# One-core decoder layer on Trainium2: where the gate products, the tile plan and the expert registers stand

## What is computed

```python
x = x + recurrence(layernorm(x))                     # stage A
x = x + cross_attention(layernorm(x), ctx)           # stage B: 16 heads, 77 keys
xf = layernorm(x)
gate_scores = xf @ gate_W + gate_b                   # [tokens, 4]
topk_scores, topk_idx = top_k(gate_scores, 2)
weights = softmax(topk_scores)
expert = LN(relu(LN(xf @ W1[e] + b1[e])) @ W2[e] + b2[e])    # stage C, for each e
x = x + sum_k weights[k] * expert[topk_idx[k]](xf) + xf
```

## Time and profile before

| what | value |
|---|---|
| median of 3 runs | 1238.64 us (1235.35 to 1240.6) |
| the profiled execution, its own time | 1244.41 us |
| its span, first to last instruction | 1242.6 us |
| PE busy | 1177.0 us, 95% of the span |
| DVE, ACT, POOL busy | 930.3, 731.6, 455.7 us |
| mean granted TensorE clock | 0.975 |

### The profile page before, as it was taken

The page is one execution under the profiler, slowest core; times in us unless marked ns, Lnnn a source line. Parts: engine busy times, 40 slices in busy tenths (PEclk is TensorE's granted clock), DMA queues, the critical chain, the costliest instruction groups (busy, mean ns, idle before and its releaser), DMA issues.

```text
span 1242.6 us, 24523 instructions
## 1 busy us (share of the span) xinstructions
PE 1177.0 (95%) x6041; PEld 991.0 (80%) x6042; DVE 930.3 (75%) x2196; ACT 731.6 (59%) x2114; POOL 455.7 (37%) x410
## 2 busy tenths in 40 slices
PE   6999999999879999999999989987999999999993
PEld 5878888888768888888888867866888888888882
DVE  6888888887745777877878676666777777777773
ACT  4323333233457758676676662655777777777773
POOL 4030000000033323545445254355655555555542
PEclk9999999999979999999999898899999999999997
DMA  8664544444620113041131325888555444444432
GB/s 273 209 161 144 194 160 152 169 152 165 200 69 1 44 60 103 11 136 67 35 103 42 129 40 127 299 225 226 86 86 82 83 84 84 81 80 84 84 65 38
DMA packets 76069, 143.90 MB, mean 116 GB/s; under 512 B 20460, under 2 KB 24752, under 8 KB 74117
## 3 DMA queue, kind: packets, MB, share of 16 engines
q1 hardware_dynamic: 56704, 101.60, 25.0%
q0 software_dynamic: 18464, 39.14, 17.3%
q10 hardware_dynamic: 837, 2.41, 0.6%
HBM read 78.83 MB, written 67.83 MB: 118 GB/s over the span
## 4 chain that ended last, share of the span: by engine, by line
PE 72%; DVE 9%; issue 8%; DMA 5%; ACT 2%; POOL 2%; DVEq 1%; another core or an unknown queue 0%; POOLq 0%; ACTq 0%; SPq 0%
PE banks L1049 26%; PE banks L670 13%; PE banks L735 6%; PE banks L875 6%; PE banks L865 5%; DMA out<-rows,scatter_rows 4%; PE banks L834 4%; PE banks L851 3%; PE banks L891 2%; PE banks L1077 2%; PE banks L1061 2%; DVE operands L1486 2%; DVE rows L1557 2%; PE banks L883 1%; DVE rows L1570 1%
## 5 line engine op out<-in xcount | busy, mean ns | idle before, releaser
L1049 PE MATMUL banks<-operands 128*128 x1608 | 392.3, 399 | 18.3 <-DVE operands L1486 11.7
L1049 PEld LDWEIGHTS banks<-operands 128*128 128x128 f32 x1608 | 299.9, 190 | 82.9 <-DVE operands L1486 14.4
L670 PE MATMUL banks<-operands 128*128 128x512 f32 (+2 forms) x1224 | 294.0, 397 | 3.6 <-DVE operands L1486 3.6
L670 PEld LDWEIGHTS banks<-operands 128*128 128x128 f32 (+1 forms) x1224 | 228.5, 194 | 49.4 <-DVE operands L1486 3.8
L1486 DVE TENSOR_TENSOR operands<-banks,operands 128x512 fp32r<-128x512 f32 (+3 forms) x328 | 218.6, 683 | 53.3 <-ACT operands L1141 48.7
L1141 ACT ACTIVATE operands<-banks 128x512 fp32r<-128x512 f32 (+3 forms) x328 | 192.1, 607 | 111.9 <-PE banks L865 45.2
L1262 ACT ACTIVATE rows<-banks,score_shift 128x77 f32<-128x77 f32 x512 | 162.3, 372 | 29.6 <-DVE score_shift L1708 28.9
L1141 ACT ACTIVATE operands<-rows 128x512 fp32r<-128x512 f32 (+3 forms) x79 | 55.2, 708 | 168.5 <-DVE rows L1557 135.4
L1411 ACT ACTIVATE banks<-banks,param_cols 128x128 f32<-128x128 f32 x268 | 99.0, 429 | 86.1 <-PE banks L1077 84.1
L2457 POOL DMA_INDIRECT out<-rows,scatter_rows x67 | 106.6, 1590 | 112.1 <-DVE rows L2196 68.8
L2381 POOL TENSOR_TENSOR rows<-rows,score_rec 128x1232 f32<-128x1232 f32 x32 | 72.0, 2252 | 157.9 <-DVE score_rec L1716 157.9
(11 more groups left out here) (178 smaller groups left out, 1718.2 us busy)
## 6 DMA issues: line engine op xcount, KB each, us to landing
expert_parts<-operands SPq DMA_DIRECT2D x32, 512.0 KB, 3.4
operands<-expert_parts SPq DMA_DIRECT2D x8, 2048.0 KB, 10.1
rows<-in_x SPq DMA_DIRECT2D x8, 1024.0 KB, 5.8
rows<-in_L_ffn_W SPq DMA_DIRECT2D x32, 256.0 KB, 3.8
x_rows<-rows SPq DMA_DIRECT2D x8, 1024.0 KB, 4.3
rows<-x_rows SPq DMA_DIRECT2D x8, 1024.0 KB, 6.0
xf_rows<-rows SPq DMA_DIRECT2D x32, 256.0 KB, 2.5
out<-rows SPq DMA_DIRECT2D x32, 256.0 KB
```

What stands on the lines that cost most here:

```text
L670: last = nc.tensor.matmul(dst, stationary(a, k), moving(b, k), start=(t == 0 and k == 0), stop=(t == len(terms) - 1 and k == n_k - 1))
L1049: last = nc.tensor.matmul(dst, stationary[:, a, k, :], weights[:, bass.ds(e, 1), w, a2, k, :].rearrange("p e f -> p (e f)"), start=False, ...
```

## The change

It has five parts.

1. In every turn from 1 to 6 the gate products of tiles 0 and 1 stand ahead of the queries of head group 3 instead of behind them, and those of tile 2 right behind these queries.
2. In the last turn the gate of chunk 6 was one block of 16 instructions at the end. Now tile 0 stands there, and tiles 1, 2 and 3 between halves of the first two projections of the tail. The group `g` moves from `MM_LAST` to `TAIL`, behind `o0`, so `o1` and the groups behind it change banks, and `prime(m1_bank[1])` waits for the read of `r` instead of `o3`. On DVE `gate_bias` and `choose` of that chunk move behind the first `x2_rows` of the tail.
3. In tile 0 of stage C the gate products of chunk 7 are two blocks of 8 instructions, the second within the first product of tile 2.
4. `plan_early(1)` moves on DVE from the start of the last turn to just before `plan_early(2)`.
5. The experts of tiles 0 to 2 are read into registers early: on PE in the last turn, on ACT ahead of its first fill. On DVE those reads move from tile 1 to tile 0.

```diff
-        MM_LAST = "o0 o1 r v0 o2 v1 o3 v2 v3 g".split()
+        MM_LAST = "o0 o1 r v0 o2 v1 o3 v2 v3".split()
...
-        TAIL = {id(T_ORDER): "xf0 xf1 xf2 xf3".split(), id(MM_ORDER): "o0 o1 o2 o3 r".split()}
+        TAIL = {id(T_ORDER): "xf0 xf1 xf2 xf3".split(), id(MM_ORDER): "o0 g o1 o2 o3 r".split()}
...
-        def tiles_of(engine, tile):
-
-
-            around = [None] * 2
+        def tiles_of(engine, tile, known=()):
+
+
+            around = [None] * 2 + list(known)
...
-            def project(c, at, j):
-
-                mm_free(at, f"o{j}")
-                for m in range(KC):
+            def project(c, at, j, parts=range(KC)):
+
+                if 0 in parts:
+                    mm_free(at, f"o{j}")
+                for m in parts:
...
-                last.then_inc(mm_done, 1)
+                if KC - 1 in parts:
+                    last.then_inc(mm_done, 1)
...
                 probs_to_keys(c, 3, (0, 1))
+                if back:
+                    gate_scores(c, (0, 1))
                 queries(c + 1, c, 3)
                 if back:
-                    gate_scores(c, (0, 1))
+                    gate_scores(c, (2,))
                 probs_to_keys(c, 3, (2,))
-                if back:
-                    gate_scores(c, (2,))
                 scores(c + 1, 1, (0, 1))
...
                 probs_to_keys(c, 3, (2,))
+                pe.wait_ge(plan_ready, 1)
+                first_experts.extend(expert_at(pe, i) for i in range(3))
                 xf_to_features(c - 1, c, 2)
...
-                gate_scores(c)
+                gate_scores(c + 1, (0,))
...
-            def first_product(i, u, e):
+            def first_product(i, u, e, between=None):
...
                 expert_product(m1_bank[u], e, 0, xT, (0, 1))
+                if between is not None:
+                    gate_products(tail_bank, tail, between).then_inc(tail_gate_done, 1)
                 pe.wait_ge(cx_lo, i + 1)
...
-                    gate_products(tail_bank, tail, range(TPC)).then_inc(tail_gate_done, 1)
+                    gate_products(tail_bank, tail, range(2))
...
             last_turn(last)
-            for j in range(TPC):
+            project(last, tail, 0, (0, 1))
+            gate_scores(tail, (1,))
+            project(last, tail, 0, (2, 3))
+            gate_scores(tail, (2,))
+            project(last, tail, 1, (0, 1))
+            gate_scores(tail, (3,))
+            project(last, tail, 1, (2, 3))
+            for j in range(2, TPC):
                 project(last, tail, j)
             positions(last - 1, tail, "r")
-            pe.wait_ge(plan_ready, 1)
-            first_product(0, 0, expert_at(pe, 0))
+            first_product(0, 0, first_experts[0])
...
-            pe.wait_ge(mm_read, mm_num(tail, "o3") + 1)
+            pe.wait_ge(mm_read, mm_num(tail, "r") + 1)
             prime(m1_bank[1])
-            first_product(1, 1, expert_at(pe, 1))
+            first_product(1, 1, first_experts[1])
...
             act.wait_ge(primed, 1)
-            fill_first(0, 0, expert_at(act, 0))
+            first_experts = [expert_at(act, i) for i in range(3)]
+            fill_first(0, 0, first_experts[0])
...
-                plan_early(1)
                 x2_rows(c - 1, c, 0)
...
                 read_positions(c)
+                plan_early(1)
                 plan_early(2)
...
                 slots(c - 2, c, aside=1)
-                gate_bias(c)
-                choose(c - 1, c)
...
                     count(NCH - 1)
+                    coming()
...
             x2_rows(last, tail, 0)
+            gate_bias(tail)
+            choose(last - 1, tail)
             count(last - 1)
```

More of the change, by code:

```diff
@@ L898, in gate_scores @@
                     mm_free(at, "g")
-                last = gate_products(mb(at, "g"), at, tiles)
+                last = gate_products(mb(at, "g"), NCH - 1 if isinstance(at, int) and at == NCH else at, tiles)
                 if tiles[-1] == TPC - 1:
@@ L1111, in c_tile @@
                 if after >= 2:
-                    first_product(i + 2, u, experts[4])
+                    first_product(i + 2, u, experts[4], range(2, TPC) if early == 0 else None)
                 second_product(i, u, experts[2], (i + 1, 1 - u) if 1 <= after < 3 else None)
@@ L1119, in _ @@
             last, tail = NCH - 1, NCH
+            first_experts = []
             last_turn(last)
-            for j in range(TPC):
+            project(last, tail, 0, (0, 1))
[6 more added lines that the diff above has]
+            for j in range(2, TPC):
                 project(last, tail, j)
             positions(last - 1, tail, "r")
-            pe.wait_ge(plan_ready, 1)
-            first_product(0, 0, expert_at(pe, 0))
+            first_product(0, 0, first_experts[0])
             for j in range(2):
                 xf_to_features(last, tail, j)
-            pe.wait_ge(mm_read, mm_num(tail, "o3") + 1)
+            pe.wait_ge(mm_read, mm_num(tail, "r") + 1)
             prime(m1_bank[1])
-            first_product(1, 1, expert_at(pe, 1))
+            first_product(1, 1, first_experts[1])
             for j in range(2, TPC):
@@ L1133, in _ @@
             rows_in(1, 0)
-            pe.wait_ge(mm_read, mm_num(tail, "r") + 1)
-            tiles_of(pe, c_tile)
+            tiles_of(pe, c_tile, first_experts)
         @block.scalar
@@ L1472, in _ @@
             act.wait_ge(primed, 2)
-            fill_first(1, 1, expert_at(act, 1))
+            fill_first(1, 1, first_experts[1])
             hidden_norm(0, 0)
@@ L1476, in _ @@
             act.wait_ge(b2_in, 16)
-            tiles_of(act, c_tile)
+            tiles_of(act, c_tile, first_experts)
             weighed_be2((NSLOT - 1) // 2, (NSLOT - 1) % 2, expert_at(act, NSLOT - 1))
```

## The result

The changed kernel takes 1254.46 us (median of 4 runs, 1252.34 to 1255.65), the kernel before 1239.42 (4 runs, 1235.35 to 1240.6): ratio 1.0125, 95% interval 1.0098 to 1.0152. It is slower by 15 us, outside my range.

The account below looks back on a forecast made before the run. PE bounds the turns, chains between engines the last turn and tail, DMA waits the first tiles. From the median 1238.6 the terms (+4.0, -2.2, -0.4, +0.5, -2.0) sum to -0.1: 1238.5 us, range 1230 to 1246.

Parts of the forecast that it names:

- The wait in the turns: Turns 2 to 6: PE's moved gate products wait for DVE's out_lo, 0.5 us each in 2 to 5, 2.0 in 6: +4.0 us.
- The slower rival: Turn 6: the new wait makes the clock fall in every run, 5.1 us more, 1243.6 to 1245.6 us; chance 0.14.
- The clock in turn 6: Turn 6: most runs lack the profiled clock fall; its absence gives -5.1 us against the profiled execution, 0 against the median.
- Gate of the tail: Tail: with chunk 6's gate in four pieces the clock fall in the 48 projection matmuls should go, -2.2 us.
- Registers: Last turn: PE's three early register reads, where it waits 0.64 us for xf, cost +0.5 us.
- Plan later: Last turn: moving the plan's eight DVE operations from ahead of x2_rows gives -0.4 us, 0 to -0.8.
- First tiles: Start of the tiles: register reads removed from ACT, PE and DVE give -2.0 us, bounds -5.5 and 0.

Follow-up runs that it names:

- e9: Kernel before with only an added PE wait, ahead of the queries of head group 3, until DVE has read the gate's bank: 1253.9 us, ratio 1.0132.
- e13: e9 with DVE's score maximum and output low parts moved ahead of the plan's first part and routing weights, so PE finds the bank free: 1236.7 us, ratio 1.0002.
- e8: Changed kernel with only DVE's score maximum and output low parts moved ahead of routing weights and the plan's first part: 1240.1 us, ratio 1.0030.
- e3: Kernel before with the new gate and query order in the turns, and DVE's maximum and low parts ahead of plan and weights: 1235.6 us, ratio 0.9984.
- e1: Kernel before with only the new order of gate and queries in turns 1 to 6: 1246.73 us, ratio 1.0063.
- e2: Changed kernel with the turns' old order put back; tail, tile 0, plan and registers stay changed: 1241.96 us, ratio 1.0025.
- e4: Kernel before with only DVE's score maximum and output low parts moved ahead of plan and routing weights: 1240.98 us, ratio 1.0033.
- e5: Kernel before with only PE's plan wait and three register reads moved into the last turn: 1240.37 us, ratio 1.0039.
- e6: Kernel before with only the tail's gate of chunk 6 in four pieces, and what goes with it on DVE: 1239.02 us, ratio 1.0023.
- e14: Kernel before with the added PE wait ahead of the queries of head group 3 in turn 5 alone: 1237.99 us, ratio 0.9996.
- e7: Changed kernel with DVE's maximum and low parts ahead of weights and plan, the plan's second part and PE's reads in their old places: 1237.0 us, ratio 1.0008.
- e12: Changed kernel run once more, unaltered, for a second trace, timed against the kernel before: 1251.15 us, ratio 1.0114.
- e10: Kernel before with the new gate order, and DVE's maximum and low parts ahead of plan and weights, in turn 6 alone: 1236.9 us, ratio 0.9999.
- e11: e10 with the gate of chunk 6 in the tail in four pieces as well: 1236.22 us, ratio 1.0001.

## Why the prediction was wrong, step by step

- **The wait in the turns, +4.0 us: right as a wait, wrong as a price.** It is 0 in turn 1, 0.44 to 0.58 in turns 2 to 5 and 2.07 in turn 6, against my 0, 0.5 and 2.0. The failed step is "with 0.5 us each, 2.0 us": it treated a wait of half a microsecond as costing its length. What stood behind it cost more, +3.2 by the falls in turns 3 and 4 (shown: e9 has the falls with the gate in its old place, e13 has none without the idle time, e8 takes the turns' falls out of the changed kernel) and +3.3 in X, 2.3 of which is the order (e3). The remaining 1.0 in X stands in turns 3 and 4 of both traces of the changed kernel and not in e1. It matches DVE's two waits for "remote" there (0.57 + 0.47 us), which no other trace has between turns 1 and 6; what they wait for stays open.
- **The slower rival** had this mechanism (the wait costs the clock), at 0.14, and only in turn 6. I set it aside for a stretch with 1.31 us of idle time in which the clock stayed at 1.00. One stretch without a fall was no evidence: turns 2 and 5 have none here either. The rule I weighed, that transposes don't count as busy in the same way (the Trainium skill, "TensorE: Matmul & The Clock Gate", Part 4), is not tested: e9 and e13 have the same transposes and differ by the idle time. The same page of the Trainium skill, section "A second HAM failure mode: psum-queue depth-cycling", tells of another kernel in which short idle stretches between groups of matmuls, frequent ones, made the clock swing. e9 against e13 agrees in that short idle stretches are enough, here 0.5 to 0.8 us once in a turn of 51 us.
- **The clock in turn 6, 0 against the median: wrong.** The seven other traces of the old order show what I took for an accident: 15.74, 14.64, 14.65, 14.66, 15.64 in e2, e4, e5, e6 and e13; 16.72 in e9 with the wait on top; in e14 the stretch behind turn 6 has a fall instead. That the profiled execution lay 5 us over the median was no proof of where. The changed order did lose this fall without the wait (11.51 in e3, e7 and e8), and with it got one of its own behind 2.07 us of idle time: 15.20.
- **Gate of the tail, -2.2 us.** Against a trace with the fall it is -1.5. But the whole block keeps its clock in three of nine traces. The mean of the nine is 24.1 us, that of the three with four pieces alone 24.0: nothing gained. The failed step is "with the gate in four pieces between groups of six wide matmuls the fall should go", priced at 2.2 us: the fall does go, but the block did not bring it each time, and the pieces cost 1.7 us themselves.
- **Registers, +0.5 us on PE: under-priced.** PE's idle time ahead of xf goes from 0.64 to 1.66 us (1.0), of which 0.3 shows in the tail with four pieces (e8 and e12 against e7) and 0.8 with the whole block (e5 against e1 and e14); in two of four traces the clock falls in the attention product behind it, 1.5 more.
- **Plan later, -0.4 us: right.** The three last stretches take 30.20 in e8, against 30.79 in e7 and 30.77 in e3 with the plan in its old place: -0.6.
- **First tiles, -2.0 us: not found.** The times from the first product to the end are 470.3 to 478.8 us in eleven traces with the old tile 0, mean 474.6, and 474.2 to 479.0 in five with the new one, mean 477.3. ACT's wait of 2.10 us ahead of its fill of tile 2 is gone, as predicted, and 1.84 us of it are back ahead of its first fill, where I had 1.4. Where the rest may go is in ACT's rows of the changed kernel, 11 us behind the fill of tile 2:

```profile
797.69 0.78 ACT L1441 ACTIVATE rows<-banks,moe_shift,moe_rstd 128x512 f32<-128x512 f32 x1 [7.79 <-DMA xf_rows<-rows]
```

This wait for a DMA is 2.19 us in the kernel before. Over the traces it is 0 to 7.42 us with the old tile 0 (mean 3.8) and 6.39 to 8.67 with the new one (mean 7.8). What makes the transfer come late no run shows, and whether the tiles really became dearer stays open: traces with the same tile 0 differ by 8.5 us from there on.

In sum, for the two traces of the changed kernel against the means of the old order: turns +8.8, turn 6 and last turn 46.0 against 45.8 (before, e2, e4, e5, e6, e13), tail 25.0 against 24.1, end 478.8 against 474.6; 14.1 of the 15 us. Of the 8.8 in the turns experiments show all but the 1.0 above. The 4.2 at the end are a difference of means that no experiment isolates. What decides in which turn half a microsecond of idle time costs the clock was not found.

## What to carry to other kernels

Ahead of moving an instruction to an earlier place on a full engine, look at whom it waits for there, and price the wait with what stands behind it: the clock, and the engines that get their input later. The mend may be on the other engine: two lines earlier on DVE gave back three quarters of this loss. A fall of the clock in a profile is not owed to the work just ahead of it until a second trace, with that work moved, lacks it; with a fall removed the next stretch may have one, so the gain has to be timed.

## What the runs showed that I had not expected

- Idle stretches of 0.56 and 0.58 us on PE, in turns that are otherwise full, are followed by a granted clock of 0.88 over 14 us; 0.44 and 0.51 us in the turns beside them by 1.00. The durations of G repeat within 0.04 us in two executions. It is no threshold: in e1 a stretch of 0.63 us is followed by 1.00 and one of 0.51 by a fall, and in e9 one of 0.76 by 1.00.
- The same wait cost 3.1 and 4.2 us by the clock with the gate products behind the queries (e9), and 1.6 each with the gate products ahead of and between them (changed).
- With a wait in turn 5 alone turn 6 kept its clock and the next stretch lost it (e14), and the same with the changed order in turn 6 alone (e10, e11).
